# Tile 1 mixed ahead of the blend of tile 2, and the last tile's second normalisation moved into the next stage

## What is computed

```python
x = x + ln(attn(ln(x)))                 # RWKV time mix and channel mix
# inside attn, on h0 = ln(x):
h  = ln(h0, ln1_w, ln1_b); xxx = h + (h - shifted(h)) * ts
k, v, r = xxx @ Wk.T, xxx @ Wv.T, sigmoid(xxx @ Wr.T)
y  = h0 + r * wkv(time_first, k, v)     # recurrence over time
h2 = ln(y, ln2_w, ln2_b)                # the second normalisation
xxx2 = h2 + (roll(h2, 1) - h2) * ts     # the mixing; row 0 takes the last time step
out = y + sigmoid(xxx2 @ Wcr.T) * (relu(xxx2 @ Wck.T)**2 @ Wcv.T)
x = x + ln(ffn(ln(x)))                  # gated ternary MLP, 128 -> 512 -> 512 -> 512 -> 128
```

## Time and profile before

| | us |
|---|---|
| median of 3 runs | 1280.5 |
| lowest, highest | 1279.04, 1280.61 |
| the profiled execution's own time | 1280.58 |
| its span | 1278.8 |
| TensorE busy in the span | 1082.7 |
| VectorE busy | 955.2 |
| ScalarE busy | 748.4 |
| GpSimd busy | 730.6 |

### The profile page before, as it was taken

One profiled execution on the slowest core, in us unless ns is written; L12 is line 12 of the kernel. 1 busy time (PEld: TensorE's weight loads), 2 busy tenths in 40 slices (PEclk: granted clock), 3 DMA queues, 4 the chain that ended last, 5 costly groups with the idle time before them and its releaser, 6 DMA issues. The chain is left out here.

```text
span 1278.8 us, 16507 instructions
## 1 busy us (share of the span) xinstructions
PE 1082.7 (85%) x4934; PEld 547.4 (43%) x4934; DVE 955.2 (75%) x1181; ACT 748.4 (59%) x1306; POOL 730.6 (57%) x640
## 2 busy tenths in 40 slices
PE   7876799999999987888989898989898388887853
PEld 3322244444444433333334333333335277776753
DVE  4898585665755439999999999999991876565545
ACT  6586545655556255767767686857653345454445
POOL 0222261431513005899898989897983167777764
PEclk8898899999999998999999999999998589999986
DMA  7000000000000003222322222222210111111225
GB/s 232 1 0 0 1 1 1 1 1 1 1 1 1 1 0 109 100 83 93 98 84 88 86 84 92 70 69 77 73 58 9 58 36 50 51 54 51 50 58 182
DMA packets 33966, 67.21 MB, mean 53 GB/s; under 512 B 7168, under 2 KB 7360, under 8 KB 33664
## 3 DMA queue, kind: packets, MB, share of 16 engines
q1 hardware_dynamic: 28464, 55.23, 13.4%
q0 software_dynamic: 4992, 10.23, 3.0%
q10 hardware_dynamic: 432, 0.76, 0.2%
HBM read 56.63 MB, written 9.57 MB: 52 GB/s over the span
## 5 line engine op out<-in xcount | busy, mean ns | idle before, releaser
L1936 POOL TENSOR_TENSOR prod<-hs,csb 128x1024 f32<-128x1024 f32 x128 | 301.9, 2359 | 125.3 <-DVE hs L1982 120.0
L1982 DVE TENSOR_TENSOR_SCAN hs<-dA,first,pD 128x1024 f32<-128x1024 f32 x128 | 300.4, 2347 | 5.2 <-DVE pD L1995 0.8
L1664 PE MATMUL pY<-prod,const 128*128 128x512 f32 x512 | 241.5, 597 | 5.0 <-POOL prod L1936 5.0
L1809 ACT ACTIVATE dA<-dt,negA 128x511 f32<-128x511 f32 x256 | 169.4, 712 | 1.5 <-DVE dt L2037 1.4
L1995 DVE TENSOR_TENSOR pD<-dtu,pD 128x1024 f32<-128x1024 f32 x128 | 154.9, 1211 | 10.0 <-ACT pD L1824 9.7
L1664 PEld LDWEIGHTS pY<-prod,const 128*128 128x128 f32 x512 | 97.5, 192 | 109.9 <-issue 92.2
L2471 POOL DMA_INDIRECT g<-moe_rows,source x78 | 82.4, 1056 | 55.5 <-DVE source L2666 26.7
L2717 DVE SCALAR_TENSOR_TENSOR hid<-pR,silu 128x512 f32<-128x512 f32 x78 | 53.9, 692 | 67.2 <-ACT silu L2425 67.2
L1162 ACT ACTIVATE stage<-pR,vec 128x512 f32<-128x512 f32 x64 | 43.9, 687 | 99.7 <-PE pR L891 99.5
L2490 POOL DMA_INDIRECT moe_outs<-y,to x78 | 81.1, 1039 | 26.2 <-issue 22.8
L1824 ACT ACTIVATE pD<-first 128x1 f32<-128x1 f32 x128 | 21.6, 169 | 119.4 <-PE pD L1674 98.2
(11 more groups left out here) (477 smaller groups left out, 2588.1 us busy)
## 6 DMA issues: line engine op xcount, KB each, us to landing
csb<-ssm_c SPq DMA_DIRECT2D x128, 256.0 KB, 3.1
raw<-moe_w SPq DMA_DIRECT2D x12, 512.0 KB, 4.8
room<-moe_outs SPq DMA_DIRECT2D x8, 512.0 KB, 8.3
hidw<-hid_w SPq DMA_DIRECT2D x1, 2048.0 KB, 10.0
moe_rows<-xt SPq DMA_DIRECT2D x8, 256.0 KB, 2.0
outT<-X SPq DMA_DIRECT2D x8, 256.0 KB, 2.0
X<-xT SPq DMA_DIRECT2D x3, 512.0 KB, 4.1
g<-moe_rows,source POOLq DMA_INDIRECT x78, 2.6
```

The source lines that it names most:

```text
L1664: last = nc.tensor.matmul(YB[c][:], G.ident, prod[:, slot(b, n), c, :], start=n == 0, stop=n == DST - 1)
L1809: last = nc.scalar.activation(dA[:, slot(b, n), c, 1:N], dt[:, b, c, 1:N], ACT.Exp, scale=negA[:, c, n:n + 1])
L1936: nc.gpsimd.tensor_tensor(prod[:, slot(b, n), :, :], hs[:, slot(b, n), :, :], csb[:, slot(b, n), :, :].to_broadcast([P, CB, N]), ALU.mult)\
L1982: nc.vector.tensor_tensor_scan(hs[:, slot(b, n), :, :].rearrange("p c n -> p (c n)"), dA[:, slot(b, n), :, :].rearrange("p c n -> p (c n)" ...
```

## The change

In the first stage `next_mixing` of both rows moves from the last tile's work into tile 2's, between `ln2_scale(1)` and `differences(2)`. All that follows from it moves up by one place: the first two key products stand ahead of `values(3)`, their Relus ahead of `carry_sums(2)`, and of the eight squares each pair stands one scan earlier, the last pair ahead of `numerators(3)`. `ln2_centre`, `ln2_square` and the others no longer run for the last tile. In the second stage's first body they return as `last_centre` (TensorE, behind step 3), `last_square` (ScalarE, behind step 4), `last_variance` (TensorE, behind step 6), `last_inverse_root` (ScalarE, behind step 7, between two table loads) and `last_scale` and `wrap` (VectorE, ahead of the groups); they use the M and Y banks and the buffer sgate3, and some products of the head now wait for them. The centring of w3 moves from behind step 3 to behind step 1, its high part from step 5 to 2, its low part from step 7 to 4. ScalarE begins the stage with a Silu of one column.

```diff
@@ -378,7 +374,7 @@
                 if t + 1 < NT:
                     keys(t + 1)
                 else:
-                    next_keys(0, range(FC))
+                    next_keys(0, (2, 3))
                 if t >= 1:
                     ln2_centre(t - 1)
                 if t == NT - 1:
@@ -390,6 +386,8 @@
                 if t + 2 < NT:
                     centre(t + 2)
                     variance(t + 2)
+                if t == NT - 2:
+                    next_keys(0, (0, 1))
                 if t + 1 < NT:
                     values(t + 1)
             next_keys(1, (2, 3))
@@ -400,14 +398,9 @@
             for b in range(B):
                 next_centre_A(b)
                 next_variance_A(b)
-            next_centre_B(0)
-            ln2_centre(NT - 1, (0,))
-            next_variance_B(0)
-            next_centre_B(1)
-            ln2_variance(NT - 1, (0,))
-            ln2_centre(NT - 1, (1,))
-            next_variance_B(1)
-            ln2_variance(NT - 1, (1,))
+            for b in range(B):
+                next_centre_B(b)
+                next_variance_B(b)
 
         @block.scalar
         def _(act):
...
@@ -525,16 +516,15 @@
             exponentials(0, S["argB"], S["factors"])
             for t in range(NT):
                 if t == NT - 1:
-                    next_relus(0, (0, 1))
+                    next_relus(0, (2, 3))
                 log_of_sums(t)
                 if 1 <= t < NT - 1:
                     ln2_square(t - 1)
                 if t == NT - 1:
-                    next_relus(0, (2, 3))
+                    next_relus(1, (0, 1))
                 exponentials(t, S["argD"], S["decays"])
                 if t == NT - 1:
                     ln2_square(t - 1)
-                    next_relus(1, (0, 1))
                 if t >= 1:
                     ln2_inverse_root(t - 1)
                 if t == NT - 1:
@@ -551,6 +541,8 @@
                     exponentials(t + 1, S["argB"], S["factors"])
                 if t + 2 < NT:
                     square(t + 2)
+                if t == NT - 2:
+                    next_relus(0, (0, 1))
                 if t + 1 < NT:
                     carry_sums(t)
                 if t + 2 < NT:
@@ -558,14 +550,9 @@
             for b in range(B):
                 next_square(b, S["h_centredA"], S["h_squaredA"])
                 next_inverse_root(b, S["h_varianceA"], S["h_logA"], S["h_rstdA"])
-            next_square_B(0)
-            ln2_square(NT - 1, (0,))
-            next_inverse_root_B(0)
-            next_square_B(1)
-            ln2_inverse_root(NT - 1, (0,))
-            ln2_square(NT - 1, (1,))
-            next_inverse_root_B(1)
-            ln2_inverse_root(NT - 1, (1,))
+            for b in range(B):
+                next_square_B(b)
+                next_inverse_root_B(b)
 
         @block.gpsimd
         def _(pool):
...
@@ -749,20 +736,21 @@
                 clip_steps(t + 1)
                 if t >= 1:
                     ln2_scale(t - 1)
+                if t == NT - 2:
+                    for b in range(B):
+                        next_mixing(b)
                 differences(t)
                 blend(t)
 
             t = NT - 1
-            next_mixing(0)
+            next_squares(0, (0, 1))
             sums(t)
-            next_mixing(1)
-            next_squares(0, (0, 1))
+            next_squares(0, (2, 3))
             distances(t)
-            next_squares(0, (2, 3))
+            next_squares(1, (0, 1))
             weigh_values(t)
-            next_squares(1, (0, 1))
+            next_squares(1, (2, 3))
             numerators(t)
-            next_squares(1, (2, 3))
             ln2_scale(t - 1)
             differences(t)
             next_residual(0)
@@ -772,10 +760,6 @@
                 next_add(b)
             for b in range(B):
                 next_normalise(b)
-                ln2_scale(t, (b,))
-            dve.wait_ge(S["scaled2"], NT * B)
-            for b in range(B):
-                nc.vector.tensor_copy(G2[:, b, 0:1], G2[:, b, T:T + 1])
 
 
 def phase_ffn(nc, G):
...
@@ -935,6 +920,17 @@
                 pe.wait_ge(S["squaredC"], at(t, b))
                 nc.tensor.matmul(Y[b][:], G.ones, sq[:, b, :], start=True, stop=True).then_inc(S["varianceC"], 1)
 
+            def last_centre():
+                for b in range(B):
+                    nc.tensor.matmul(M[b][:], G.centre, XA[:, b, ds(NT - 1)], start=True, stop=True).then_inc(S["centredL"], 1)
+
+            def last_variance():
+                for b in range(B):
+                    pe.wait_ge(S["squaredL"], b + 1)
+                    if b:
+                        pe.wait_ge(S["w3_low"], 1)
+                    nc.tensor.matmul(Y[1 - b][:], G.ones, last_sq[:, b, :], start=True, stop=True).then_inc(S["varianceL"], 1)
+
             def head_after(t, g, first):
                 if first and g == 0:
                     pe.wait_ge(S["w_low"], ATT)
@@ -942,19 +938,23 @@
                     if (b, f) == (0, 0):
                         pe.wait_ge(S["hidden"], nth(t - 1, B - 1, FC - 1))
                     elif (b, f) == (0, 1):
-                        if not first:
+                        if first:
+                            pe.wait_ge(S["logL"], B)
+                        else:
                             pe.wait_ge(S["logC"], at(t - 2, 1))
                     else:
                         pe.wait_ge(S["squares"], nth_ahead(t, b, f) - (1 if b and f else 2))
                     key_product(t, b, f, key_bank(b, f))
                 if g in (2, 3):
-                    if not first:
+                    if first:
+                        pe.wait_ge(S["scaledL"], g - 1)
+                    else:
                         pe.wait_ge(S["scaledC"], at(t - 2, g - 2))
                     gate(t, g - 2)
                 if g == 4:
                     if first:
                         pe.wait_ge(S["w_low"], CV)
-                        pe.wait_ge(S["w3_low"], 1)
+                        pe.wait_ge(S["logL"], B)
                     values(t, 0)
                 if g == 5:
                     centre_A(t, 0)
...
@@ -994,8 +994,12 @@
                         if i == 1 and not first:
                             for c in range(B):
                                 variance_C(t - 1, c)
+                        if i == 1 and first:
+                            centre_w3()
                         if i == 3 and first:
-                            centre_w3()
+                            last_centre()
+                        if i == 6 and first:
+                            last_variance()
                 for g in range(GROUPS):
                     layer, b, o = group(g)
                     if first and b == 0 and o == 0:
...
+            def last_square():
+                for b in range(B):
+                    act.wait_ge(S["centredL"], b + 1)
+                    nc.scalar.activation(last_sq[:, b, :], M[b][:], ACT.Square).then_inc(S["squaredL"], 1)
+
+            def last_inverse_root():
+                for b in range(B):
+                    act.wait_ge(S["varianceL"], b + 1)
+                    nc.scalar.activation(last_sq[:, b, :], Y[1 - b][:], ACT.Ln, bias=G.eps_c).then_inc(S["logL"], 1)
+                    act.wait_ge(S["logL"], b + 1)
+                    nc.scalar.activation(last_sq[:, b, :], last_sq[:, b, :], ACT.Exp, scale=-0.5).then_inc(S["rstdL"], 1)
+
             def body(t, first, last_):
                 if not first:
                     for b in range(B):
@@ -1145,12 +1161,17 @@
                                              scale=col("w1_s", f)).then_inc(S["silus"], 1)
                         if first and i < len(weights):
                             weights_high(i)
-                        if first and i == len(weights):
+                        if first and i == 2:
                             high_w3()
+                        if first and i == 4:
+                            last_square()
                 if not first:
                     act.preload_act_table_set("natural_log_exp_and_others")
                     for b in range(B):
                         inverse_root_C(t - 1, b)
+                else:
+                    act.preload_act_table_set("natural_log_exp_and_others")
+                    last_inverse_root()
                 act.preload_act_table_set("gelu_and_others")
                 for g in range(GROUPS):
                     layer, b, o = group(g)
@@ -1165,6 +1186,7 @@
 
             act.wait_ge(G.ffn_loaded, 64)
             act.wait_ge(S["scales"], 1)
+            nc.scalar.activation(last_sq[:, 0, 0:1], G.zero_c, ACT.Silu)
             for t in range(NT):
                 body(t, t == 0, t == NT - 1)
             act.preload_act_table_set("natural_log_exp_and_others")
...
                 here, earlier = (bass.ds(P2_ORDER[t] * N + shift, N) for shift in (1, 0))
+                if P2_ORDER[t] == 0:
+                    dve.wait_ge(S["wrapped"], B)
                 for b in rows_:
...
```

(23 more changed lines are left out.)

22 lines of the change are left out of this document (7 added, 15 removed).

## The result

The changed kernel took 1284.42 us (median of 7 runs, 1282.05 to 1285.28) beside 1280.61 us for the kernel before (7 runs, 1279.04 to 1281.88): ratio 1.0032, 95% interval 1.0022 to 1.0043. Its profiled execution took 1283.09 us. That is 7.0 us above the forecast and outside its range. Of all executions in this document, four had a far lower mean clock (0.902 at most) and took 1300.56 us or more, two of them in before_head; medians and comparisons leave them out.

What follows compares the result with a forecast made beforehand. In the part changed, 97 to 190 us, VectorE was read as the bound, hardly pausing. From the profiled 1280.58 us, terms -1.5, -2.1 and +0.4 gave 1277.4 us, range 1274.9 to 1280.2.

Steps and rivals of the forecast that it cites:

- the clock term: First stage's end: TensorE's low clock after a 3.0 us idle spell takes back 1.6 us of the gain.
- part 1: Mixing ahead of the blend, late first stage: -3.1 + 1.6 = -1.5 us, bounds -3.1 and +0.3.
- the quiet mixing: VectorE, first stage: both mixings run with GpSimd idle, 1.22 us each to the next start; VectorE 2.3 us ahead.
- needs 7.3 us: GpSimd, tile 2: begins at 103.6, needs 7.3 us, so the tile's output is whole at 110.9.
- I take the short one: TensorE, first stage's end: the clock is low for 3.4 us rather than 6.8 us, costing 1.6 us.
- rival (b): First stage's end: the clock stays low for 6.8 us, part 1 gives +0.3, time 1279.2 us; chance 0.13.
- Part 2: End of the first stage: the last tile's second normalisation leaves it, -2.1 us, bounds -1.6 and -2.6.
- Part 3: Second stage's first body: the moved normalisation and one more table load enter, +0.4 us, bounds -1.3 and +3.4.
- Rival (e): Second stage: a table switch blocks ScalarE for about twice its 1.28 us, time 1280.0 us; chance 0.03.
- Rival (d): First stage: clock falls near 110.4, not back before row 1's last key products; +1.8 us, time 1282.4; chance 0.06.
- From 190 us on nothing changes, and the shift is carried through: Rest of the span after the second stage's first body: no change, so the earlier gain reaches the end whole.
- About 0.2%, 2.6 us, is what a measurement of this kernel can tell: Whole kernel: smallest difference a measurement can tell from no change, 2.6 us, with the line at 1277.9 us.

Runs made afterwards that it cites:

- before_head: Kernel before with five more keep-busy products ending the third stage and three large products at the fourth stage's head, copy still on VectorE: 1279.90 us (10 runs).
- after_halo_dense_2: Changed kernel with the three-column copy on ScalarE and added TensorE products around the fourth stage's head, run once more: 1267.81 us (4 runs).
- before_again: The kernel before, unchanged, profiled a second time: 1280.63 us (12 runs).

## Why the prediction was wrong

From the forecast to the measured median there are 7.0 us. Up to the first scan the change took off 1.0 us, counted from the clip, where 3.2 were forecast: +2.24. The earlier start gave -2.25, the third stage +6.55, what is behind it -0.83, and the median lies 1.33 us above the profiled execution. What failed of the prediction's own steps is the clock term of part 1, and the step that carries the shift unchanged from 190 us to the end.

- **Part 1, the quiet mixing**: right. VectorE's share came as priced, 0.53 us and 1.24 us to the next start.
- **Part 1, "needs 7.3 us"**: GpSimd started where forecast (101.39 + 2.25 = 103.64, forecast 103.6) but needed 7.96 us, 101.39 to 109.35. I took its time from the tile before, where the four operations took 1.64, 2.07, 2.20 and 1.27 us; now they took 1.65, 2.24, 2.20 and 1.74, the last beside VectorE's distances (107.55 to 109.89), which follow the sums sooner. 0.7 us on the chain, and 0.3 more up to the variance product, which starts at 115.31 + 2.25 = 117.56 and not at 116.55.
- **Part 1, "I take the short one"**: this failed most. The 3-us idleness was seen, and so was rival (b); the clock fell for 6.8 us in six of the eight traces with the mixing moved and nothing added, twice for 3.4 us in one, and for 3.4 us in one. Only in that last one, after_halo_dense_2, did the last square come early, at 28.34. My reason, that products follow closely from there, says nothing: they do in all eight. From the variance product to the last square it took 8.06 us (115.31 to 123.37), where the sum had 5.15 and 1.6 for the clock: the term was 2.9 us. In after_halo_dense_2, with the short fall, it took 6.66 us (118.19 to 124.85), as priced; so the price was right and the choice wrong. Part 1 was +0.8 us in the first pair, not -1.5 (the clock 1.3, GpSimd 0.7 and 0.3 of steps make the 2.3 us), and +1.4 against before_again. The trace that I started from was itself a long one: its 28.91 us stand beside 28.2 to 28.3 in five of the eight traces of before's stages, so even the 28.34 gains nothing on most of them; (b) deserved the first place and not 0.13.
- **Part 2**: right. 1.61 us at the seam (2.83 to 1.22) and 0.55 us in the chain (last square to last normalisation 22.15 to 21.60), 2.2 where 2.1 was forecast.
- **Part 3**: right in the pair of traces, +0.3 for +0.4. But 20.6 us stood in five of the eight traces of before's stages for the 21.5 of mine, so against most of them it is +1.2, within its bounds.
- **Rival (e)**: refuted. Silu, load and logarithm follow at 168.20, 168.90 and 170.20, and 1.28 + 0.02 us leaves no room for the drain. The Trainium skill's figure, "ScalarE: Activation LUTs", "What ACT_TABLE_LOAD costs", isn't seen in this place.
- **Rival (d)**, the only slower one: the time was on its side and its mechanism was not there: the clock was up until 114.57 us.
- **"From 190 us on nothing changes, and the shift is carried through"**: the work doesn't change, the time does, by +6.5 us in the third stage of the first trace. The third stage varies from 469.0 to 476.0 us over eleven traces with the copy on VectorE, and the fourth's head by 7 us. In the profiled execution this outweighs all that the change did. For the median it isn't shown which part is this draw: the later medians of the same changed kernel, 1282.38 and 1280.98 us, are 5.0 and 3.6 us above the forecast too.
- **"About 0.2%, 2.6 us, is what a measurement of this kernel can tell"**: three runs within 1.6 us were taken for its noise. Single runs spread over 10 us and medians over 2.9.

## What to carry to other kernels

Before pricing a gain of 2 or 3 us, price what the unchanged rest does by itself: a small VectorE copy between SBUF tensors beside a busy GpSimd, and each place where TensorE waits 2 to 5 us, are draws that can swallow it here (the copy 0.1 to 3.7 us, the head of a stage 25 to 32). Such a copy belongs on another engine even if it seems to cost 0.2 us; here that was worth 11 us, over three times what I had forecast for the change. And where idleness of TensorE is moved, count the long fall of the clock as the likely one unless a row of the same pattern shows otherwise.

## What the runs showed of the hardware

- VectorE's copy of 128x3 took 0.14 to 3.67 us beside GpSimd; the same copy on ScalarE took 0.19 us every time. At 848.47 it was passed by three GpSimd instructions that started behind it.
- GpSimd is slowed as well: the same addition of 128x512 (XA) took 1.32 and 2.24 us, the longer one beside VectorE's scans.
- The granted clock is not the same from execution to execution of one program: from 0.937 to 0.950 in its mean over the span in 35 runs, 3.7 us in time between the upper and the lower part of them.
- A load of ScalarE's table between two functions cost 1.28 to 1.30 us in the place read here (168.90 us), nothing more.
